# Copying the high parts of the split weights into PSUM on TensorE, with three weight loads in flight

## The reference

```python
fm = emb_table[jnp.arange(N_CAT)[None, :], cat_idx]      # 26 rows of 128 per sample
h = jax.nn.relu(dense_x @ Wd1 + bd1)                      # 13 -> 512
h = jax.nn.relu(h @ Wd2 + bd2)                            # -> 256
dense = jax.nn.relu(h @ Wdf + bdf)                        # -> 128
Z = jnp.concatenate([fm, dense[:, None, :]], axis=1)      # 27 vectors
S = jnp.einsum('bie,bje->bij', Z, Z)
x = jnp.concatenate([S[:, iu, ju], dense], axis=-1)       # 351 pairs + 128
x = jax.nn.relu(x @ Wt1 + bt1)                            # -> 1024
x = jax.nn.relu(x @ Wt2 + bt2)                            # -> 1024
x = jax.nn.relu(x @ Wt3 + bt3)                            # -> 512
x = jax.nn.relu(x @ Wt4 + bt4)                            # -> 256
return jax.nn.sigmoid(x @ Wo + bo)
```

## Time and profile before

| | us |
|---|---|
| median of three runs | 172.91 (172.88 to 172.96) |
| the profiled execution's own time | 174.08 |
| its span from first to last instruction | 172.3 |
| PE busy | 160.7 |
| POOL busy | 99.5 |
| DVE busy | 70.5 |
| ACT busy | 66.8 |

### The profile page before, as it was taken

How to read it: one execution, slowest core, us unless ns; L and a number is a source line. 1 busy time by engine, 2 the same in 40 slices (tenths; PEclk the granted TensorE clock), 3 DMA queues, 4 the chain that set the end, 5 groups by cost and what they waited for, 6 DMA issues and landing times.

```text
span 172.3 us, 3924 instructions
## 1 busy us (share of the span) xinstructions
PE 160.7 (93%) x1703; PEld 115.7 (67%) x1703; DVE 70.5 (41%) x139; ACT 66.8 (39%) x117; POOL 99.5 (58%) x111
## 2 busy tenths in 40 slices
PE   1999999676699999999999999999999999999995
PEld 1334355423377878778777887777878777788993
DVE  4005258863557456462512144245032262322230
ACT  3367688764658576433103033411111331201202
POOL 3777777777777777777777777777777000000000
PEclk9999999999999999999999999999999999999999
DMA  3999755566799562222122121212222000000000
GB/s 54 288 388 293 181 173 169 177 181 180 203 366 309 157 175 86 65 50 58 49 56 53 50 61 49 61 46 49 62 49 61 15 4 0 0 4 0 0 0 0
DMA packets 6674, 18.18 MB, mean 106 GB/s; under 512 B 2309, under 2 KB 2441, under 8 KB 6530
## 3 DMA queue, kind: packets, MB, share of 16 engines
q1 hardware_dynamic: 3330, 11.12, 20.5%
q0 software_dynamic: 3328, 6.82, 15.4%
HBM read 17.93 MB, written 0.00 MB: 104 GB/s over the span
## 4 chain that ended last, share of the span: by engine, by line
PE 72%; DMA 24%; ACT 1%; DVE 1%; issue 0%
PE mp L489 27%; DMA w<-in_wt 23%; PE mp L514 10%; PE mp L456 10%; PE tp L464 6%; PE gp L415 5%; PE gp L405 5%; PE gp L533 3%; PE tp L550 3%; DMA idx<-in_cat_idx 1%; PE mp L558 1%; PE gp L427 1%; ACT w2h L635 1%; PE gp L573 0%; PE tp L541 0%
## 5 line engine op out<-in xcount | busy, mean ns | idle before, releaser
L350 POOL DMA_INDIRECT rows<-in_emb,row_of x104 | 98.6, 948 | 33.3 <-issue 30.2
L489 PE MATMUL mp<-w2l,a1h 128*128 128x512 f32 x64 | 26.7, 418 | 0.0
L489 PE MATMUL mp<-w2h,a1h 128*128 128x512 f32 x64 | 26.1, 408 | 0.0
L489 PE MATMUL mp<-w2h,a1l 128*128 128x512 f32 x64 | 25.4, 396 | 0.0
L405 PE MATMUL gp<-ident,rows 128*128 128x128 f32 x104 | 16.7, 275 | 3.2 <-DMA rows<-in_emb,row_of 3.2
L661 ACT COPY zt<-gp 128x512 f32<-128x512 f32 x16 | 9.4, 586 | 25.3 <-PE gp L405 25.1
L405 PEld LDWEIGHTS gp<-ident,rows 128*128 128x128 f32 x104 | 12.8, 140 | 9.4 <-DMA rows<-in_emb,row_of 5.2
L851 DVE TENSOR_TENSOR raw<-mp,bc 128x512 f32<-128x512 f32 x8 | 5.5, 691 | 26.5 <-PE mp L489 26.5
L415 PEld LDWEIGHTS gp<-zt 128*32 128x32 f32 x1024 | 11.1, 110 | 7.0 <-issue 6.6
L802 DVE TENSOR_TENSOR w2l<-w,tp 128x1024 fp32r<-128x1024 f32 x7 | 8.5, 1218 | 14.2 <-ACT tp L646 14.2
L489 PEld LDWEIGHTS mp<-w2h,a1l 128*128 128x128 f32 x64 | 12.1, 189 | 2.8 <-DVE a1l L845 0.8
(11 more groups left out here) (89 smaller groups left out, 246.3 us busy)
## 6 DMA issues: line engine op xcount, KB each, us to landing
w<-in_wt SPq DMA_DIRECT2D x13, 512.0 KB, 4.6
rows<-in_emb,row_of POOLq DMA_INDIRECT x104, 3.0
w<-in_wt SPq DMA_DIRECT2D x3, 468.0 KB
bc<-in_rows SPq DMA_DIRECT2D x1, 1024.0 KB, 6.2
wd_sb<-in_wd SPq DMA_DIRECT2D x1, 512.0 KB, 3.6
w1d<-in_wt SPq DMA_DIRECT2D x1, 512.0 KB, 6.9
bt<-in_rows SPq DMA_DIRECT2D x1, 512.0 KB, 9.4
wdf_sb<-in_wdf SPq DMA_DIRECT2D x1, 128.0 KB, 3.1
```

The source lines that it names most:

```text
L350: pool.indirect_dma_start(out=rows[:, n % RING, :], out_offset=None, in_=emb.rearrange("c v e -> (c v) e"), in_offset=bass.IndirectOffsetO ...
L489: last = pe.matmul(sums_of(t, 2 + h), a[:, k, :], w[:, k, cols], start=(k == 0 and part == 0), stop=(k == M1 - 1 and part == 2))
```

## The change

TensorE, and no longer ACT, fills `tp` for chunks 3 to 10: two products of an fp32r identity (`ident_r`, a rounded copy of `ident` that ACT makes at the start) with the rounded chunk (`w1h`, `w2h`), 512 columns each. Each waits for ACT's `high_part` of the chunk (`w_hi`) and for DVE's split of the chunk before (`w_lo`). For chunks 0 to 2 ACT still fills `tp`. The last w2 chunk is split whole like the others, before layer 1; only the eight halves of w3 are left for `mp`, four through bank 1 before the second half of layer 2 and four through bank 0 before layer 3, none in layer 3. SP keeps three loads in flight. In the front dense products 3 to 6 move ahead of feature group 5 (the sixth), and one `keep_warm(512)` is gone.

```diff
+IN_FLIGHT = 3
...
-WHOLE_SPLITS = LOADS_12 - 1
+WHOLE_SPLITS = LOADS_12
...
-SPLITS += [("w2", M1 - 1, h * 512, 512) for h in range(2)]
...
-                sp.wait_ge(w_in[n - (2 if n < 5 else 1)], 16)
+                if n >= IN_FLIGHT:
+                    sp.wait_ge(w_in[n - IN_FLIGHT], 16)
...
-                    pe.wait_ge(w_lo, SPLITS_H1)
+                    pe.wait_ge(w_lo, len(SPLITS))
...
+            def middle_part(n):
+
+                name, k = LOADS[n]
+                high = w1h[0:PC, k, :] if name == "w1" else w2h[:, k, :]
+                rows_of = PC if name == "w1" else P
+                pe.wait_ge(ident_cast, 1)
+                pe.wait_ge(w_hi, n + 1)
+                pe.wait_ge(w_lo, n)
+                for h in range(2):
+                    last = pe.matmul(tp[:, h, :], ident_r[0:rows_of, :], high[:, h * 512:(h + 1) * 512], start=True, stop=True)
+                last.then_inc(w_mid, 1)
...
-                sc.copy(high, weights)
+                sc.copy(high, weights).then_inc(w_hi, 1)
...
+            sc.copy(ident_r[:], ident[:]).then_inc(ident_cast, 1)
...
             features(0, 0)
-            split_hi(3)
+            high_part(3)
             features(0, 2)
-            split_hi(4)
+            high_part(4)
+            high_part(5)
             features(0, 4)
-            split_hi(5)
-            split_hi(6)
-            split_hi(7)
+            for n in range(6, 10):
+                high_part(n)
             features(0, 6)
-            split_hi(8)
-            high_part(9)
+            high_part(10)
             pairs_out(0)
-            middle_part(9)
```

More of the change, by code:

```diff
@@ L71 @@
 LOADS_12 = PAIR_CHUNKS + M1
-WHOLE_SPLITS = LOADS_12 - 1
+IN_FLIGHT = 3
+WHOLE_SPLITS = LOADS_12
 SPLITS = [(name, k, 0, TOP[1]) for name, k in LOADS[:WHOLE_SPLITS]]
-SPLITS += [("w2", M1 - 1, h * 512, 512) for h in range(2)]
 SPLITS += [("w3", k, 0, 512) for k in range(M2)]
 SPLITS_1 = 1 + SPLITS.index(("w1", 2, 0, TOP[1]))
-SPLITS_H0, SPLITS_H1 = WHOLE_SPLITS + 4, WHOLE_SPLITS + 8
+SPLITS_H0 = WHOLE_SPLITS + M2 // 2
 def split_of_w2(k):
@@ L151, in build @@
         ident = sb("ident", [P, P])
+        ident_r = sb("ident_r", [P, P], F32R)
         row_of = sb("row_of", [P, TILES * BLOCKS], I32)
@@ L206, in build @@
         pre_out = sem("pre_out")
+        w_hi = sem("w_hi")
+        ident_cast = sem("ident_cast")
         w_lo = sem("w_lo")
@@ L281, in split_bank @@
             if n >= WHOLE_SPLITS:
-                return mp[:, 0 if SPLITS_H0 <= n < SPLITS_H1 else 1, :]
+                return mp[:, 1 if n < SPLITS_H0 else 0, :]
             rows_of = PC if SPLITS[n][0] == "w1" else P
@@ L495, in layer_3 @@
                 if t == 0:
-                    pe.wait_ge(w_lo, SPLITS_H1)
+                    pe.wait_ge(w_lo, len(SPLITS))
                 for n in range(PRODUCTS_3):
-                    if t == 0 and n == 3 * SPLITS[SPLITS_H1][1]:
-                        pe.wait_ge(w_lo, len(SPLITS))
                     for g in FEATURES_3[t].get(n, ()):
@@ L584, in _ @@
             pe.wait_ge(w1d_in, 16)
-            for m in range(2):
-                dense_products(m)
+            dense_products(0)
+            dense_products(1)
+            middle_part(3)
             transpose_features(0, 2)
@@ L590, in _ @@
             dense_products(2)
+            middle_part(4)
             grams(0, 1)
             transpose_features(0, 4)
-            for m in range(3, 5):
-                dense_products(m)
+            dense_products(3)
+            middle_part(5)
+            dense_products(4)
+            middle_part(6)
+            dense_products(5)
+            middle_part(7)
+            dense_products(6)
+            middle_part(8)
             transpose_features(0, 5)
-            dense_products(5)
+            dense_products(7)
             grams(0, 2)
-            dense_products(6)
-            dense_products(7)
+            middle_part(9)
+            transpose_features(0, 6)
             pe.wait_ge(pre_out, 7)
-            keep_warm(512)
-            transpose_features(0, 6)
             keep_warm(256)
             transpose_features(0, 7)
+            middle_part(10)
             grams(0, 3)
@@ L728, in _ @@
                 if t == 0:
-                    high_part(WHOLE_SPLITS)
-                    middle_part(WHOLE_SPLITS)
+                    high_part(LOADS_12)
                 for n in range(PRODUCTS_2):
@@ L734, in _ @@
                         if t == 0:
-                            middle_part(WHOLE_SPLITS + 1)
-                            high_part(LOADS_12)
-                            middle_part(WHOLE_SPLITS + 2)
-                            middle_part(WHOLE_SPLITS + 3)
+                            middle_part(WHOLE_SPLITS)
+                            high_part(LOADS_12 + 1)
+                            for k in range(WHOLE_SPLITS + 1, SPLITS_H0):
+                                middle_part(k)
                     for g in FEATURES_2[t].get(n, ()):
@@ L742, in _ @@
                     if n == PRODUCTS_2 // 2 - 1 and t == 0:
-                        high_part(LOADS_12 + 1)
+                        high_part(LOADS_12 + 2)
                         middle_part(SPLITS_H0)
-                        high_part(LOADS_12 + 2)
+                        high_part(LOADS_12 + 3)
                     if n == TURN_2:
@@ L748, in _ @@
                         if t == 0:
-                            middle_part(SPLITS_H0 + 1)
-                            middle_part(SPLITS_H0 + 2)
-                            middle_part(SPLITS_H0 + 3)
-                            high_part(LOADS_12 + 3)
+                            for k in range(SPLITS_H0 + 1, len(SPLITS)):
+                                middle_part(k)
                 for n in range(PRODUCTS_3):
@@ L879, in _ @@
             dense_products_out(2)
-            split_lo(4)
-            dense_products_out(3)
-            dense_products_out(4)
-            split_lo(5)
+            for n in range(4, 8):
+                split_lo(n)
+                dense_products_out(n - 1)
+            split_lo(8)
             features(0, 5)
-            dense_products_out(5)
-            split_lo(6)
-            dense_products_out(6)
-            split_lo(7)
             dense_products_out(7)
+            split_lo(9)
             features(0, 7)
+            split_lo(10)
             turn_sums(0)
-            split_lo(8)
             pairs_lo(0)
-            split_lo(9)
             for t in range(TILES - 1):
@@ L905, in _ @@
                     if n == TURN_1B:
-                        if t == 0:
-                            split_lo(WHOLE_SPLITS)
                         layer_1_lo(t, 1)
                         if t == 0:
-                            for k in range(WHOLE_SPLITS + 1, SPLITS_H0):
+                            for k in range(WHOLE_SPLITS, SPLITS_H0):
                                 split_lo(k)
@@ L922, in _ @@
                         if t == 0:
-                            for k in range(SPLITS_H0 + 1, SPLITS_H1):
+                            for k in range(SPLITS_H0 + 1, len(SPLITS)):
                                 split_lo(k)
```

10 lines of the change are left out of this document (removed).

## The result

| | median (lowest to highest), us | runs | profiled execution, us | its span |
|---|---|---|---|---|
| before | 172.89 (172.85 to 172.96) | 4 | 174.08 | 172.3 |
| after | 176.63 (176.48 to 177.75) | 4 | 176.48 | 174.7 |

The change makes the kernel slower by 3.7 us: ratio 1.0198, 95% interval 1.0147 to 1.0249. The sign and the mechanism are those of the forecast; the time is 1.8 us above the forecast's middle and 0.03 above the 176.6 that its range ends at, so it lies on the very edge. The change forecast was 1.9 us, about half of what was measured.

The account below looks back on a forecast made before the run. The prediction took TensorE as bound from 46 us on, so layer 1's start in tile 0 sets the end. It summed + 1.4 (later layer 1) and + 0.5 (layer 2 stall) to + 1.9, 174.8 us; range 172.9 to 176.6.

Parts of the forecast that it names:

- The line and its 18.5: Front of tile 0: alternating TensorE copies and DVE splits, 2.05 us a chunk, put layer 1 18.5 us after feature group 4's start.
- Where s lies: s is the start of tile 0's feature group 4, taken as 29.1 us, so layer 1 at 47.6, 1.4 later.
- the rival of starving gathers: Front: queued loads push gather lag past 6.4 us; at 8 us s is 31.7 and the time 177.4; 8 in 100.
- The two bounds: On group 4's start: TensorE's own line, not before 28.5 us, and the seventeenth gather's landing, between 27.0 and 30.1.
- The loads: Front: three loads in flight, one per 1.8 us, bring chunk loads in by about 31, all landed by 33 us.
- The stall in layer 2: Middle of tile 0's layer 2: TensorE waits 0.5 us for four w3 halves through bank 1; bounds 0.3 and 0.7.
- from one execution to the median: Final sum: the 1.9 us worked out against the profiled execution's span of 172.3 is added to the median, giving 174.8.
- upper bound of + 3.7: Upper end of the case: group 4 at 30.1, stall 0.7 and hand-overs 0.1 dearer.
- hand-over: Between TensorE and DVE over the one `tp`: split 1.22, copy 0.71 and 0.12 for the ways, 2.05 us a chunk.
- the first rival: Front: the line is less tight and earlier loads pay, at most 0.9 us because of the last gather: 172.0; 8 in 100.
- The clock: Rival: TensorE falls to the slower clock in its waits between 30 and 44 us, about + 3, 176; 3 in 100.

Follow-up runs that it names:

- Doubled copies: The changed kernel with each of TensorE's eight copies into `tp` made twice, four products in place of two; 179.30 us, ratio 1.0347.
- the early rounding: The changed kernel with ACT's rounding of chunk 10 moved ahead of its features of group 6; 176.68 us, ratio 1.0164.
- the two chunks put behind: The changed kernel with copies and splits of chunks 9 and 10 put behind the row sums; 177.26 us, 175.39 with the w3 loads held back.
- the repetition: The changed kernel itself, unaltered, timed and profiled again in turn with the kernel before; 176.62 us, ratio 1.0182.
- the second trace of before: The unaltered kernel before, profiled once more; median 173.38 us, profiled execution 173.83 us.
- two loads: The changed kernel with two weight loads in flight in place of three; 177.88 us in one execution.
- w3 was held back: w3 loads issued only after DVE's first transpose of the sums: changed kernel 176.40 us, with the early rounding 175.61, with two chunks behind the sums 175.39.
- the old loads: The changed kernel with weight loads issued as in the kernel before, two, then one in flight; 181.33 us in one execution.

## Why the prediction was right, and where it was off

**The line and its 18.5.** Right. Predicted: copies 2.05 apart, waits of 0.7 for DVE; measured 2.11 and 0.55 to 0.68. Predicted over 1 us of waiting for ACT ahead of the last copy; measured 1.13. Predicted layer 1 at s + 18.5; measured s + 18.6. Doubled copies, the early rounding and the two chunks put behind each move it the way the line says, once the stop is out of the way: by 2.5 (2.3 expected), 0.7 (0.9 to 1.1) and 1.7 (about 2).

**Where s lies.** Right: 29.1 predicted, 29.38 measured. The seventeenth gather, issued at 23.84, was the one that TensorE waited for until then, 5.4 us after its issue; gathers from 9 to 16 us took 6.9, more than the 6.4 that the rival of starving gathers starts from, but the lag had fallen again by the time of this one. By the Trainium skill's rule (DMA: Bandwidth & Descriptors, section Queues, rings and completion order) that rows are served in turn, which would leave the landing at 3.3, s would have been 28.5; the row speaks for the deeper queue costing something. But the gather does not always decide. In the repetition group 4 starts at 28.43 without waiting for it, so that it had landed within 4.7 us; of the nine executions of the changed front with three loads in flight four wait for the gather there (0.35 to 1.23 us), and in the other five TensorE's own line ends last. The two bounds are that close, and the agreement of 29.1 with 29.38 is partly luck. The start varies from 28.43 to 29.56 (30.20 with doubled copies).

**The loads.** All landed by 33 was predicted; the last was issued at 29.52 and took 5.8, so 35.3. One per 1.8 us was too fast for the stretch in which the gathers take their share. It cost nothing, since ACT rounds that chunk at 42.3.

**The stall in layer 2.** 0.5 predicted, 0.18 measured; and the same distance, 13.26, stands in the second trace of before, without a stall. The term is smaller than the difference between two executions. The mechanism is visible (PEld waits for DVE's split), its size was taken too high, in three small steps: the fourth split ended 13.2 after layer 1 (60.46 + 0.69) where the working has 13.3, its way to TensorE took 0.05 and not 0.1, and I rounded a worked 0.4 up to 0.5.

**The term that failed: from one execution to the median.** The working sums against the profiled execution of before (span 172.3) and comes to + 1.9; the trace of after gives + 2.4, of which 1.7 at layer 1 (1.4 predicted), 0.2 in layer 2 and 0.45 in tiles 2 and 3, which differ by as much between traces of one kernel. So far it is off by 0.5. It then adds the 1.9 to the median 172.91, and this step lost 1.3, or 0.8 if 173.41, the median of before over 17 runs, is taken. The profiled execution was 1.2 above its median because its chain of single loads had ended late. In the second trace that chain isn't in the path: layer 1 starts at 44.68, and TensorE waits for gathers instead. The medians on the floor speak for typical executions being like it or better. A TensorE line that doesn't depend on that chain (18.6 behind s) is to be set against that typical execution. From the second trace of before to after it is: group 4 + 0.9, from there to layer 1 + 2.4 (18.6 - 16.2), and from layer 1 to tile 1's last group - 0.6, mostly the 0.49 that the gathers had taken; together 2.7, the difference of the spans. That second execution is itself 0.4 to 0.9 above the medians of its kernel (173.83; 173.41 to 172.89); 2.7 and these make 3.1 to 3.6 of the 3.2 to 3.7. That this last part is the distance to the floor is worked out, and not seen in a trace of a 172.9 run.

**Luck in the range.** Its upper bound of + 3.7 was made of a late group 4 (s = 30.1), a stall of 0.7 and dearer hand-overs. None of the three came: s was 29.38, the stall 0.18 and a hand-over only 0.06 dearer. The range reached 176.6 for reasons that did not occur, and what filled it was the step above, which had no bound of its own.

**The same step in the first rival.** It let earlier loads gain at most 0.9, "136.2 less 135.3", and took that off the median: 172.0. Those 0.9 are the profiled execution's distance to the gathers' floor, and the median had already used them up. Three loads in the kernel before gave 1.000 as ratio.

**The clock.** This rival stood at 3 in 100, on the ground that a wait of 1.6 us had not cost the clock. It doesn't decide the median, but it is real in single executions, and before has them too: it makes 1.0 to 1.3 us in each run of after, of its repetition and of the two chunks behind that shows a mean clock of 0.99. One trace in which a wait is harmless says little about the next.

## What to carry to other kernels

When the profiled execution isn't on the median, find out what was late in it before adding anything to the median, and work each term out against what bounds the typical run. Room below a floor that was read from one slow execution may already be used up in the median. Moving a cheap copy to an engine that "has time" puts that engine into a line with its consumer if there is only one buffer between them, and everything behind it in program order waits too. When removing a wait gives nothing, look for a second hold that ends at the same time, and remove both before giving up either explanation.

## What the hardware did that I had not expected

**TensorE can wait for its own instructions.** In five executions with w3's loads where the change has them (after, its repetition, early rounding, two loads, two chunks behind the sums), TensorE stopped for 0.16 to 1.93 us at the same place of its program, and went on 2.3 to 2.4 us after a 16 KB packet of the instruction queue had started (42.51 to 43.01 us). That is 0.7 to 1.9 us behind the start of feature group 7. In the four executions in which w3 was held back the packet started at 40.5 to 41.0, 0.6 to 1.3 us ahead of group 7, and there was no stop. With doubled copies the packet is behind group 7 too (45.73, 0.9 behind), and TensorE, which is slower to the same place there, has no stop. Put by the place, TensorE's 342nd product: in the eleven executions of the changed kernel and its variants it never starts less than 2.3 us behind the packet's start. It starts 2.3 to 2.4 behind where there is a stop, 2.3 with doubled copies, 2.6 to 3.5 with w3 held back, 5.6 with the old loads. The Trainium skill (Runtime: NRT & Kernel Launch, section Instruction fetch mechanics) says that the sequencer fetches the next 16 KB ahead of use and that the cost is mostly hidden; here it was not, and the stop depended on what else the DMA engines were carrying. How the loads delay the fetch is not shown; the traces have the packet's start and not its request. One thing speaks for waiting: with w3 held back the packet starts 0.1 to 0.6 us after TensorE's 269th product, and in the seven where loads are in flight 1.7 to 3.3 us after it. That the request goes by this place is inferred.

**A stop of under 1 us can be followed by several us at 1.2 GHz** (0.50 granted from 46 to 48 us behind a stop of 0.86), and in other executions one of 1.14 us is not. What decides between them stayed open.
